# First block normalised by VectorE, first weight piece split in halves, two low parts moved to GpSimd

## The chip, the cores and the metric

One core of a Trainium2 chip runs the whole program in one launch. Its engines run side by side, each in the order of its own instruction list, and wait for each other by semaphores: TensorE (PE, with its weight loads as PEld), VectorE (DVE), ScalarE (ACT), GpSimd (POOL) and the queue of SyncE (SP), which issues most of the transfers. GpSimd issues transfers of its own. The metric is the device time in microseconds (us) of one execution, as the median of several runs.

## The reference

The program is one macaron layer on 4096 tokens (2 x 2048) of width 512: half a mixture-of-experts feed-forward, a state-space (Mamba-2) layer, and half a feed-forward again with the same weights.

```
x = x + 0.5 * ffn(layernorm(x))      # called "a" below
x = x + mamba(layernorm(x))          # "m"
x = x + 0.5 * ffn(layernorm(x))      # "b"

def ffn(x):                          # 64 experts of width 128, 4 per token, at most 64 tokens each
    scores = softmax(x @ router_w.T);  pick 4 per token;  gather, silu(gate) * up, down, scatter-add
    sg, su = x @ sh_gate_w, x @ sh_up_w               # shared part, width 2 x 512 = 1024
    return routed + (silu(sg) * su) @ sh_down_w
```

The change touches only the beginning of the first feed-forward.

## The kernel before, in words

Float32 products are made of three TensorE passes. Each operand is kept as a high part (a ScalarE copy into a reduced type) and a low part (the difference, one subtraction); `three` (L766 to L769) adds high times high, high times low and low times high.

**Stages of the first feed-forward.** Tokens of the shared part go in 16 blocks of 256 (`BS`), those of the router in 8 blocks of 512 (`BR`). The shared weights, 128 x 12288, arrive in six pieces of 128 x 2048, in the order 0, 1, 4, 2, 3, 5; a piece is known here by its place o in that order. Every piece lands in one of three staging buffers (`stage`, o = 0 to 5 use buffers 0, 1, 2, 0, 1, 2), ScalarE makes its high part (`split`, L610 to L616), VectorE its low part (`split`, L968 to L971), and only then may SyncE load the next piece into the same buffer (`load_piece`, L404 to L408).

**Start.** SyncE loads the first rows, piece 0, further rows, the router weights, pieces 1 and 2 and the block `xs` 0. VectorE takes mean and variance of the first 256 rows (`norm_first(0)`), GpSimd their inverse deviation (`inv_std`), and ScalarE normalises them in two passes per tile, one for the mean and one for the scale (`normed`, L618 to L635). TensorE turns them (`turn_s`), ScalarE and VectorE make the two parts of the turned rows (`turned_s`), and the first products of gate and up follow (`gate_or_up`). The engines' lists at the start read, in order:

```
SP    rows 0a, piece 0, rows 0b, router, pieces o = 1, 2, xs 0, pieces o = 3, 4, 5, xs 1, xr 1
ACT   split(0), normed(0), turned_s x2, split(1), split(2), split(3), r_both, silu(0), turned_r(0,0),
      split(4), split(5), product_hi(0), turned_r(0,1), silu(1), turned_r(0,2), ...
DVE   norm_first(0), split(0), turned_s x2, split(1), norm_first(1), norm_apply(0), split(2), split(3),
      r_both, product(0), turned_r(0,0), split(4), split(5), product_lo(0), turned_r(0,1), turned_r(0,2), ...
PE    turn_s x2, gate(0), up(0), turn_r(0,0), turn_r(0,1), logits(0,0), gate(1), turn_r(0,2), logits(0,1), up(1), ...
POOL  constants, zeros, inv_std(0) x2, the clearing of slot_rows (waits for all six low parts), inv_std(1), ...
```

**Router rows.** `norm_apply` makes the normalised rows `hr` of a router block. TensorE turns them in four groups into one PSUM tile `p_x0` (`turn_r`), so that group k + 1 waits until ScalarE and VectorE have read group k (`turned_r`, both engines; TensorE waits for `htr_ready`).

**The clearing.** GpSimd issues one transfer of 8336 KB of zeros into `slot_rows` (L543) once all low parts are made.

The second feed-forward runs the same code with `prior` set; its early part is interleaved with the end of the state-space layer. Semaphores of the first feed-forward are used again there.

## Time and profile before

| | |
|---|---|
| time, median of 3 runs | 2319.41 us (2318.42 to 2331.59) |
| span of the profiled execution, first to last instruction | 2318.1 us |
| TensorE busy | 2261.7 us (98%) |
| VectorE busy | 1364.6 us (59%) |
| ScalarE busy | 883.8 us (38%) |
| GpSimd busy | 692.8 us (30%) |
| mean granted TensorE clock | 0.992 |
| chain that ended last | TensorE 87%, DMA 7%, VectorE 3% |

The profiled execution is one of its own; its span is the time from its first to its last instruction, 1.3 us below the median of the runs. Busy time counts instructions that compute; a matmul's end is modelled, so successive matmuls overlap in the records and their pitch, the distance of their starts, tells more than their durations. In a timeline row stand the start, the time from that start to the end of the row's last instruction, the engine and line, what is written from what, how many instructions were merged, and in brackets the engine's idle time before it with what ended it.

### The profile page before, as it was taken

How to read it: one execution, taken by the hardware profiler on the slowest of the kernel's cores; microseconds unless marked ns; L12 is line 12 of the kernel's file. 1: busy time of each engine (PE TensorE's matmuls, PEld its weight loads, DVE VectorE, ACT ScalarE, POOL GpSimd, SP SyncE). 2: the span in 40 equal slices, each digit the busy share in tenths (PEclk: the TensorE clock that was granted, in tenths of full speed). 3: DMA queues.
4: the chain of work that ended last, by engine and by line, in shares of the span. 5: the costliest groups of instructions: out<-in, count | busy, mean ns of one | idle time of the engine just before them, and what ended most of it. 6: DMA issues, size and time to landing. Idle time of an engine off the chain costs nothing.

```text
span 2318.1 us, 41268 instructions
## 1 busy us (share of the span) xinstructions
PE 2261.7 (98%) x16412; PEld 1999.8 (86%) x16412; DVE 1364.6 (59%) x3200; ACT 883.8 (38%) x1562; POOL 692.8 (30%) x534
## 2 busy tenths in 40 slices
PE   6999999999999999999999999999999999999996
PEld 6999999777798899989889988998989999777785
DVE  6777762222327777777777777778776763223221
ACT  5232221233336455445455555555322221233230
POOL 1244443112221333333222232321144444112131
PEclk9999999999999999999999999999999999999998
DMA  8876424999854111111111111114385623889948
GB/s 268 267 256 217 154 93 156 304 277 284 245 112 134 39 28 28 29 28 28 29 28 28 28 29 34 32 41 154 134 294 186 224 75 106 310 275 286 280 81 175
DMA packets 129279, 334.73 MB, mean 144 GB/s; under 512 B 24450, under 2 KB 45186, under 8 KB 118400
## 3 DMA queue, kind: packets, MB, share of 16 engines
q1 hardware_dynamic: 80592, 236.63, 28.6%
q0 software_dynamic: 48496, 95.46, 18.2%
q8 instruction: 131, 2.15, 0.4%
q14 instruction: 60, 0.49, 0.1%
HBM read 218.25 MB, written 172.77 MB: 169 GB/s over the span
## 4 chain that ended last, share of the span: by engine, by line
PE 87%; DMA 7%; DVE 3%; issue 1%; ACT 1%; SPq 0%; POOLq 0%; DVEq 0%; POOL 0%; ACTq 0%
PE m_p_ab L1679 5%; PE m_p_ab L1680 4%; PE m_p_ab L1681 4%; DMA out<-b_y,b_row_no 4%; PE m_p_x L1679 3%; PE m_p_x L1681 3%; PE m_p_x L1680 3%; PE p_up_a L767 3%; PE p_x_a L871 3%; PE m_p_y L1799 2%; PE p_gate_a L767 2%; PE m_p_y L1800 2%; PE p_up_a L769 2%; PE p_up_a L768 2%; PE p_gate_a L768 2%; PE p_gate_a L769 2%
## 5 line engine op out<-in xcount | busy, mean ns | idle before, releaser
L1995 DVE SCALAR_TENSOR_TENSOR m_xt<-m_ssm,m_convw,m_xt 128x256 f32<-128x256 f32 x384 | 212.0, 565 | 57.7 <-ACT m_ssm L1546 48.5
L503 POOL DMA_INDIRECT slot_rows<-a_hr,a_slot_now x128 | 128.5, 1004 | 141.5 <-PE p_gate_a L769 91.5
L503 POOL DMA_INDIRECT slot_rows<-b_hr,b_slot_now x128 | 128.4, 1003 | 139.4 <-PE p_gate_b L769 90.5
L1679 PE MATMUL m_p_ab<-m_ht_hi,m_wi_b_hi 128*128 128x256 f32 x576 | 163.5, 284 | 1.8 <-ACT m_ssm L1546 1.8
L1680 PE MATMUL m_p_ab<-m_ht_lo,m_wi_b_hi 128*128 128x256 f32 x576 | 160.4, 279 | 0.0
L1681 PE MATMUL m_p_ab<-m_ht_hi,m_wi_b_lo 128*128 128x256 f32 x576 | 160.3, 278 | 0.0
L767 PE MATMUL p_gate_a<-a_hts_hi,a_w_hi 128*128 128x256 f32 x512 | 148.3, 290 | 1.8 <-DVE a_hts_lo L1066 1.8
L1452 POOL TENSOR_TENSOR m_state_dec<-m_state,m_etot 128x1024 f32<-128x1024 f32 x31 | 74.0, 2388 | 252.4 <-ACT m_etot L1562 252.4
L767 PE MATMUL p_gate_b<-b_hts_hi,b_w_hi 128*128 128x256 f32 x512 | 146.5, 286 | 0.4 <-DVE b_hts_lo L1066 0.4
L767 PE MATMUL p_up_a<-a_hts_hi,a_w_hi 128*128 128x256 f32 x512 | 145.6, 284 | 0.0
L767 PE MATMUL p_up_b<-b_hts_hi,b_w_hi 128*128 128x256 f32 x512 | 145.5, 284 | 0.0
L769 PE MATMUL p_gate_a<-a_hts_hi,a_w_lo 128*128 128x256 f32 x512 | 144.9, 283 | 0.0
L768 PE MATMUL p_gate_a<-a_hts_lo,a_w_hi 128*128 128x256 f32 x512 | 144.9, 283 | 0.0
L769 PE MATMUL p_gate_b<-b_hts_hi,b_w_lo 128*128 128x256 f32 x512 | 143.4, 280 | 0.0
L768 PE MATMUL p_gate_b<-b_hts_lo,b_w_hi 128*128 128x256 f32 x512 | 143.3, 280 | 0.0
L769 PE MATMUL p_up_a<-a_hts_hi,a_w_lo 128*128 128x256 f32 x512 | 143.1, 279 | 0.0
L769 PE MATMUL p_up_b<-b_hts_hi,b_w_lo 128*128 128x256 f32 x512 | 143.0, 279 | 0.0
L768 PE MATMUL p_up_a<-a_hts_lo,a_w_hi 128*128 128x256 f32 x512 | 143.0, 279 | 0.0
L768 PE MATMUL p_up_b<-b_hts_lo,b_w_hi 128*128 128x256 f32 x512 | 142.9, 279 | 0.0
L1072 DVE TENSOR_TENSOR b_prod<-b_silu,p_up_b 128x512 f32<-128x512 f32 x64 | 44.0, 688 | 155.5 <-PE p_up_b L769 154.4
L1072 DVE TENSOR_TENSOR a_prod<-a_silu,p_up_a 128x512 f32<-128x512 f32 x64 | 44.0, 688 | 139.4 <-PE p_up_a L769 138.1
L1544 ACT ACTIVATE m_xt<-m_p_ab,m_convb,m_convw 128x256 f32<-128x256 f32 x128 | 72.2, 564 | 129.2 <-PE m_p_ab L1681 129.2
(376 smaller groups left out, 7354.8 us busy)
## 6 DMA issues: line engine op xcount, KB each, us to landing
a_ew<-in_ew SPq DMA_DIRECT2D x32, 1536.0 KB, 7.7
b_ew<-in_ew SPq DMA_DIRECT2D x32, 1536.0 KB, 8.0
after_ffn<-a_zeros POOLq DMA_DIRECT2D x6, 2048.0 KB, 9.2
out<-b_zeros POOLq DMA_DIRECT2D x6, 2048.0 KB, 9.9
slot_rows<-a_zeros POOLq DMA_DIRECT2D x1, 8336.0 KB, 39.1
a_rows<-slot_rows SPq DMA_DIRECT2D x32, 260.5 KB, 8.4
b_rows<-slot_rows SPq DMA_DIRECT2D x32, 260.5 KB, 8.8
m_x<-after_ffn SPq DMA_DIRECT2D x16, 512.0 KB, 3.6
```

The costliest lines, as they stand in the source:

```text
L503: g_.indirect_dma_start(out=xg, out_offset=bass.IndirectOffsetOnAxis(ap=slot_now[r % HR][:, at:at + 1], axis=0), in_=hr[r % HR][:, j, :], ...
L767: t.matmul(out, l_hi, r_hi_, start=first, stop=False)
L768: t.matmul(out, l_hi, r_lo_, start=False, stop=False)
L769: return t.matmul(out, l_lo, r_hi_, start=False, stop=last)
L871: mm = t.matmul(p_x1[e * CAP:(e + 1) * CAP, 0:2 * F], xt[:, q % 2, k, e * CAP:(e + 1) * CAP], w[q % EU][:, e, k * 2 * F:(k + 1) * 2 * F], ...
L1072: v.tensor_tensor(prod[:, i % 2, :, :], silu[:, i % 2, :, :], p_up[:, :, :], ALU.mult).then_inc(prod_ready, 1)
L1452: g.tensor_tensor(state_dec[:], state[:], etot[:, j, :].unsqueeze(2).to_broadcast([P, NH, HP]), ALU.mult).then_inc(state_dec_ready, 1)
L1544: a.activation(xt[:, m, :], ab_of(J_SSM[m])[:, 0:BM], ACT.Identity, bias=convb[:, m:m + 1], scale=convw[:, m, HALO:CONV]).then_inc(tap_rea ...
L1679: t.matmul(out, l_hi, r_hi_, start=first, stop=False)
L1680: t.matmul(out, l_hi, r_lo_, start=False, stop=False)
L1681: return t.matmul(out, l_lo, r_hi_, start=False, stop=last)
L1995: ins_ = v.scalar_tensor_tensor(xt[:, m, :], ssm[:, m, i:i + BM], convw[:, m, i:i + 1], xt[:, m, :], ALU.mult, ALU.add)
```

## The change

ScalarE no longer normalises the first block: `normed(0)` leaves its list, and VectorE does it with one instruction per tile (`norm_shared`: subtract the mean, multiply by the inverse deviation), right after `norm_first(0)`. VectorE's subtraction for piece o = 0 is cut into two halves of 1024 columns, one before and one after its two `turned_s`; TensorE's first product waits for the first half only, its second for both. The low parts of o = 3 and o = 5 (`by_pool`) are made by GpSimd, right after the inverse deviations and ahead of the clearing; VectorE skips them. The waits on low parts count the two engines apart (`split_done`). SyncE's load of `xr` for block 1 waits for `hs_ready` in place of `hs_mid`, and the counts of `hs_mid` (`mids`) leave out the first block. For the second feed-forward `by_pool` is empty.

```
--- before.py
+++ after.py
@@ -277,6 +277,7 @@
 
         piece_loaded = [sem(f"piece_loaded{i}") for i in range(3)]
         small_loaded, w_hi_done, w_lo_done, r_split = sem("small_loaded"), sem("w_hi_done"), sem("w_lo_done"), sem("r_split")
+        w_lo_half, w_lo_pool = sem("w_lo_half"), sem("w_lo_pool")
         zeros_set, slots_cleared, acc_cleared = sem("zeros_set"), sem("slots_cleared"), sem("acc_cleared")
         xs_loaded, x_stored = [sem(f"xs_loaded{u}") for u in range(XB)], sem("x_stored")
         late_loaded = sem("late_loaded")
@@ -314,6 +315,15 @@
         norms = lambda at: at // TS + 1 if at < TR else at // TR + 2
         uses = lambda o: slot_of[:o + 1].count(slot_of[o])
 
+        by_pool = [] if prior else [3, 5]
+
+        def split_done(o):
+
+            on_pool = o in by_pool
+            return (w_lo_pool if on_pool else w_lo_done), len([e for e in range(o + 1) if (e in by_pool) == on_pool])
+
+        mids = lambda b: (own(b) - (0 if prior else 1)) * TS
+
 
         stored = lambda r: r - FROM_MEMORY[0] // 2 + 1 if 2 * r in FROM_MEMORY else 0
         own = lambda b: len([e for e in range(b + 1) if e not in FROM_MEMORY])
@@ -403,7 +413,7 @@
 
             def load_piece(o):
                 if uses(o) > 1:
-                    sp.wait_ge(w_lo_done, max(e for e in range(o) if slot_of[e] == slot_of[o]) + 1)
+                    sp.wait_ge(*split_done(max(e for e in range(o) if slot_of[e] == slot_of[o])))
                 i = order[o]
                 sp.dma_start(stage[slot_of[o]], shw[:, i * PIECE:(i + 1) * PIECE]).then_inc(piece_loaded[slot_of[o]], 16)
 
@@ -447,13 +457,14 @@
                         load_piece(o)
                         if o == 2:
                             load_xs(0)
-                    sp.wait_ge(w_lo_done, PIECES - 1)
+                    sp.wait_ge(*split_done(3))
+                    sp.wait_ge(*split_done(4))
                     load_xs(1)
                 for b in range(NS):
                     if b + 1 < NR:
                         sp.wait_ge(hr_ready, (b + 1) * TR)
                         if b == 0 and not prior:
-                            sp.wait_ge(hs_mid, TS)
+                            sp.wait_ge(hs_ready, TS)
                         sp.dma_start(xr[:], src_r[b + 1]).then_inc(xr_loaded, 16)
                     if b < NR:
                         store_turned(b, 0)
@@ -529,6 +540,11 @@
                 pool.dma_start(acc[first:first + rows, :], acc[HALF + first:HALF + first + rows, :], accum_op=ALU.add,
                                max_dma_last_dim=8192).then_inc(done, 16)
 
+            def split(o):
+                cols = slice(order[o] * PIECE, (order[o] + 1) * PIECE)
+                pool.wait_ge(w_hi_done, o + 1)
+                g_.tensor_tensor(w_lo[:, cols], stage[slot_of[o]], w_hi[:, cols].bitcast(F32), ALU.subtract).then_inc(w_lo_pool, 1)
+
             def early():
                 inv_std(0)
 
@@ -537,9 +553,12 @@
                 pool.wait_ge(zeros_set, 1)
                 if not prior:
                     inv_std(0)
+                for o in by_pool:
+                    split(o)
                 if clear_slots:
                     n = SLOTS // P
-                    pool.wait_ge(w_lo_done, PIECES)
+                    pool.wait_ge(w_lo_pool, len(by_pool))
+                    pool.wait_ge(w_lo_done, PIECES - len(by_pool))
                     pool.dma_start(xg.rearrange("(p a) d -> p (a d)", p=P).rearrange("p (n m) -> p n m", n=n),
                                    zeros[:, :].unsqueeze(1).to_broadcast([P, n, ROW])).then_inc(slots_cleared, 16)
                 inv_std(1)
@@ -581,7 +600,7 @@
                 if f.follow:
                     f.follow.pool.first()
                 add_block(NS - 3, ALL_ADDED)
-                pool.wait_ge(hs_mid, own(NS - 1) * TS)
+                pool.wait_ge(hs_mid, mids(NS - 1))
                 last = xs[:, (NS - 1) % XB, :, :]
                 pool.dma_start(last, acc_s[NS - 1], accum_op=ALU.add).then_inc(last_read, 16)
                 if merge_all:
@@ -617,10 +636,7 @@
 
             def normed(b):
                 rows_of = xs[:, b % XB, :, :]
-                if b == 0 and not prior:
-                    rows_of = xr
-                else:
-                    act.wait_ge(*loaded(b))
+                act.wait_ge(*loaded(b))
                 act.wait_ge(mean_ready, norms(b * TS))
                 act.wait_ge(rstd_ready, norms(b * TS))
                 wait(act, ts_full, 2 * own(b) - 2)
@@ -630,7 +646,7 @@
                                  bias=neg_mean[:, at:at + 1]).then_inc(hs_mid, 1)
                 for j in range(TS):
                     at = b * TS + j
-                    act.wait_ge(hs_mid, own(b) * TS - TS + j + 1)
+                    act.wait_ge(hs_mid, mids(b) - TS + j + 1)
                     a.activation(hs[:, j, :], hs[:, j, :], ACT.Identity,
                                  scale=rstd[:, at:at + 1]).then_inc(hs_ready, 1)
 
@@ -713,7 +729,6 @@
             def program():
                 if not prior:
                     split(0)
-                    normed(0)
                     turned_s(0, 0)
                     turned_s(0, 1)
                     act.wait_ge(c.built, c.BUILT)
@@ -787,10 +802,15 @@
                     else:
                         pe.wait_ge(hts_ready, 2 * own(b))
                 if g == 0 and b == 0:
-                    pe.wait_ge(w_lo_done, order.index(u) + 1)
+                    if i == 0 and not prior:
+                        pe.wait_ge(w_lo_half, 1)
+                    else:
+                        pe.wait_ge(*split_done(order.index(u)))
                 wait(pe, free, i)
                 for m in range(2):
                     n = 2 * u + m
+                    if i == 0 and g == 0 and m == 1 and not prior:
+                        pe.wait_ge(*split_done(0))
                     if g == 0 and m == 1 and turns_product(3 * i) is not None:
                         turn_prod(turns_product(3 * i))
                     for k in range(KD):
@@ -802,7 +822,7 @@
                 b, u = divmod(i, UN)
                 pe.wait_ge(act_ready, i + 1)
                 if b == 0 and u % 2 == 0:
-                    pe.wait_ge(w_lo_done, order.index(UN + u // 2) + 1)
+                    pe.wait_ge(*split_done(order.index(UN + u // 2)))
                 if u == 0:
                     wait(pe, acc_ready, b * TS)
                     if prior and b == 0:
@@ -966,9 +986,25 @@
                 dve.wait_ge(dve_step, steps[0])
 
             def split(o):
+                if o in by_pool:
+                    return
                 cols = slice(order[o] * PIECE, (order[o] + 1) * PIECE)
                 dve.wait_ge(w_hi_done, o + 1)
                 v.tensor_tensor(w_lo[:, cols], stage[slot_of[o]], w_hi[:, cols].bitcast(F32), ALU.subtract).then_inc(w_lo_done, 1)
+
+            def split_half(half):
+
+                cols = slice(half * PIECE // 2, (half + 1) * PIECE // 2)
+                dve.wait_ge(w_hi_done, 1)
+                v.tensor_tensor(w_lo[:, cols], stage[0][:, cols], w_hi[:, cols].bitcast(F32),
+                                ALU.subtract).then_inc(w_lo_done if half else w_lo_half, 1)
+
+            def norm_shared():
+
+                dve.wait_ge(rstd_ready, 1)
+                for j in range(TS):
+                    v.tensor_scalar(hs[:, j, :], xr[:, j, :], mv[:, j, 0:1], rstd[:, j:j + 1],
+                                    ALU.subtract, ALU.mult).then_inc(hs_ready, 1)
 
             def norm_stats(r):
                 if r == 0:
@@ -1138,9 +1174,11 @@
             def program():
                 if not prior:
                     norm_first(0)
-                    split(0)
+                    norm_shared()
+                    split_half(0)
                     turned_s(0, 0)
                     turned_s(0, 1)
+                    split_half(1)
                     split(1)
                     norm_first(1)
                     dve.wait_ge(c.built, c.BUILT)
```

## Rows read from the trace of the kernel before

**Rows 1.** The page: its head, then busy time, share and instructions of TensorE.
```profile
span 2318.1 us, 41268 instructions
PE 2261.7 (98%) x16412; PEld 1999.8 (86%) x16412; DVE 1364.6 (59%) x3200; ACT 883.8 (38%) x1562; POOL 692.8 (30%) x534
```

**Rows 2.** Waits of TensorE, whole span: waiter, releaser, us in total, times, longest.
```profile
PE p_ts_a L778 <- ACT a_hs L634: 11.5, 1, 11.5
PE p_x_a L823 <- DVE a_htr_lo L1008: 7.9, 4, 5.4
```

**Rows 3.** Timeline of TensorE, 14 to 36 us.
```profile
14.83 0.58 PE L767 MATMUL p_gate_a<-a_hts_hi,a_w_hi 128*128 128x256 f32 x1 [1.41 <-DVE a_hts_lo L1066]
...
28.82 1.09 PE L823 MATMUL p_x_a<-ident,a_hr 128*128 128x128 f32 x4 [5.44 <-DVE a_htr_lo L1008]
...
33.12 0.35 PE L767 MATMUL p_gate_a<-a_hts_hi,a_w_hi 128*128 128x256 f32 x1
...
34.45 0.28 PE L769 MATMUL p_gate_a<-a_hts_hi,a_w_lo 128*128 128x256 f32 x1
35.48 0.63 PE L823 MATMUL p_x_a<-ident,a_hr 128*128 128x128 f32 x4 [0.75 <-DVE a_htr_lo L1008]
```

**Rows 4.** Busy time by engine, 28 to 30 us; last three: clock, DMA share, GB/s.
```profile
28.00:30.00 2.00, 1.18 (x5) 1.21 (x6) 2.00 (x3) 0.10 (x1) 0.00 (x0) 0.50 0.55 229
```

**Rows 5.** Timeline of ScalarE, 13 to 32 us.
```profile
13.95 1.90 ACT L616 ACTIVATE a_w_hi<-a_xs 128x2048 fp32r<-128x2048 f32 x1
...
19.25 1.92 ACT L616 ACTIVATE a_w_hi<-a_hr 128x2048 fp32r<-128x2048 f32 x1 [1.60 <-DMA a_hr<-in_shw]
...
29.90 1.91 ACT L616 ACTIVATE a_w_hi<-a_hr 128x2048 fp32r<-128x2048 f32 x1 [4.08 <-DMA a_hr<-in_shw]
```

**Rows 6.** Timeline of VectorE, 15 to 35 us.
```profile
15.89 2.29 DVE L971 TENSOR_TENSOR a_w_lo<-a_xs,a_w_hi 128x2048 fp32r<-128x2048 f32 x1 [1.11 <-ACT a_w_hi L616]
...
20.75 1.92 DVE L1002 TENSOR_SCALAR a_hr<-a_xr,a_mv,a_rstd 128x512 f32<-128x512 f32 x4 [0.82 <-POOL a_rstd L495]
...
22.66 4.48 DVE L971 TENSOR_TENSOR a_w_lo<-a_hr,a_w_hi 128x2048 fp32r<-128x2048 f32 x2
...
28.00 0.68 DVE L1008 TENSOR_TENSOR a_htr_lo<-p_x_a,a_htr_hi 128x512 fp32r<-128x512 f32 x1
...
34.05 0.68 DVE L1077 TENSOR_TENSOR a_act_lo<-a_prod,a_act_hi 128x512 fp32r<-128x512 f32 x1
```

**Rows 7.** Timeline of SyncE's queue: issue of pieces o = 1 and o = 5.
```profile
3.33 0.45 SPq L408 DMA_DIRECT2D a_xs<-in_shw  x1
...
24.97 0.33 SPq L408 DMA_DIRECT2D a_hr<-in_shw  x1
```

**Rows 8.** Transfers issued from 3.2 to 3.6 us: KB each, us to landing.
```profile
a_xs<-in_shw SPq DMA_DIRECT2D x1, 1024.0 KB, 9.7
```

**Rows 9.** Timeline of GpSimd, 19 to 35 us.
```profile
19.94 0.70 POOL L495 TENSOR_TENSOR a_rstd<-a_var_eps,neg_half 128x2 f32<-128x2 f32 x1 [12.77 <-DVE a_var_eps L993]
34.46 1.87 POOL L543 DMA_DIRECT2D slot_rows<-a_zeros  x1 [13.82 <-DVE a_w_lo L971]
```

**Rows 10.** Timeline of GpSimd in the state-space layer, at 803 us.
```profile
803.43 2.64 POOL L1466 TENSOR_TENSOR m_cdec<-m_cdec,m_ct 128x1024 f32<-128x1024 f32 x1 [2.77 <-ACT m_cdec L1572]
```

**Rows 11.** Timeline of VectorE from 803.84 us.
```profile
803.86 3.01 DVE L1995 SCALAR_TENSOR_TENSOR m_xt<-m_ssm,m_convw,m_xt 128x256 f32<-128x256 f32 x2
```

**Rows 12.** Lines 1995 and 1452 alone: durations in ns, least/median/most.
```profile
L1995 DVE SCALAR_TENSOR_TENSOR m_xt<-m_ssm,m_convw,m_xt x384: 474/485/2506, 728.6 to 1571.7; 128x256 f32<-128x256 f32 x192
...
L1452 POOL TENSOR_TENSOR m_state_dec<-m_state,m_etot x31: 1899/2355/2882, 749.3 to 1551.4; 128x1024 f32<-128x1024 f32 x31
```

**Rows 13.** The page's transfers: KB each, us from issue to landing.
```profile
slot_rows<-a_zeros POOLq DMA_DIRECT2D x1, 8336.0 KB, 39.1
```

**Rows 14.** Queues from 31 to 38 us: packets, MB, share; q1 is SyncE's.
```profile
q1 hardware_dynamic: 989, 1.96, 85.9%
```

**Rows 15.** Timeline of ScalarE at 77 us.
```profile
76.98 0.60 ACT L661 ACTIVATE a_htr_hi<-p_x_a 128x512 fp32r<-128x512 f32 x1 [1.42 <-DMA turned_rows<-a_htr_lo]
```

More of the change, by code:

```diff
@@ L279, in ffn @@
         small_loaded, w_hi_done, w_lo_done, r_split = sem("small_loaded"), sem("w_hi_done"), sem("w_lo_done"), sem("r_split")
+        w_lo_half, w_lo_pool = sem("w_lo_half"), sem("w_lo_pool")
         zeros_set, slots_cleared, acc_cleared = sem("zeros_set"), sem("slots_cleared"), sem("acc_cleared")
@@ L315, in ffn, with split_done @@
         uses = lambda o: slot_of[:o + 1].count(slot_of[o])
+        by_pool = [] if prior else [3, 5]
+        def split_done(o):
+            on_pool = o in by_pool
+            return (w_lo_pool if on_pool else w_lo_done), len([e for e in range(o + 1) if (e in by_pool) == on_pool])
+        mids = lambda b: (own(b) - (0 if prior else 1)) * TS
         stored = lambda r: r - FROM_MEMORY[0] // 2 + 1 if 2 * r in FROM_MEMORY else 0
@@ L405, in load_piece @@
                 if uses(o) > 1:
-                    sp.wait_ge(w_lo_done, max(e for e in range(o) if slot_of[e] == slot_of[o]) + 1)
+                    sp.wait_ge(*split_done(max(e for e in range(o) if slot_of[e] == slot_of[o])))
                 i = order[o]
@@ L449, in program @@
                             load_xs(0)
-                    sp.wait_ge(w_lo_done, PIECES - 1)
+                    sp.wait_ge(*split_done(3))
+                    sp.wait_ge(*split_done(4))
                     load_xs(1)
@@ L455, in program @@
                         if b == 0 and not prior:
-                            sp.wait_ge(hs_mid, TS)
+                            sp.wait_ge(hs_ready, TS)
                         sp.dma_start(xr[:], src_r[b + 1]).then_inc(xr_loaded, 16)
@@ L530, in merge, with split @@
                                max_dma_last_dim=8192).then_inc(done, 16)
+            def split(o):
+                cols = slice(order[o] * PIECE, (order[o] + 1) * PIECE)
+                pool.wait_ge(w_hi_done, o + 1)
+                g_.tensor_tensor(w_lo[:, cols], stage[slot_of[o]], w_hi[:, cols].bitcast(F32), ALU.subtract).then_inc(w_lo_pool, 1)
             def early():
@@ L539, in program @@
                     inv_std(0)
+                for o in by_pool:
+                    split(o)
                 if clear_slots:
                     n = SLOTS // P
-                    pool.wait_ge(w_lo_done, PIECES)
+                    pool.wait_ge(w_lo_pool, len(by_pool))
+                    pool.wait_ge(w_lo_done, PIECES - len(by_pool))
                     pool.dma_start(xg.rearrange("(p a) d -> p (a d)", p=P).rearrange("p (n m) -> p n m", n=n),
@@ L583, in program @@
                 add_block(NS - 3, ALL_ADDED)
-                pool.wait_ge(hs_mid, own(NS - 1) * TS)
+                pool.wait_ge(hs_mid, mids(NS - 1))
                 last = xs[:, (NS - 1) % XB, :, :]
@@ L619, in normed @@
                 rows_of = xs[:, b % XB, :, :]
-                if b == 0 and not prior:
-                    rows_of = xr
-                else:
-                    act.wait_ge(*loaded(b))
+                act.wait_ge(*loaded(b))
                 act.wait_ge(mean_ready, norms(b * TS))
@@ L632, in normed @@
                     at = b * TS + j
-                    act.wait_ge(hs_mid, own(b) * TS - TS + j + 1)
+                    act.wait_ge(hs_mid, mids(b) - TS + j + 1)
                     a.activation(hs[:, j, :], hs[:, j, :], ACT.Identity,
@@ L789, in gate_or_up @@
                 if g == 0 and b == 0:
-                    pe.wait_ge(w_lo_done, order.index(u) + 1)
+                    if i == 0 and not prior:
+                        pe.wait_ge(w_lo_half, 1)
+                    else:
+                        pe.wait_ge(*split_done(order.index(u)))
                 wait(pe, free, i)
@@ L793, in gate_or_up @@
                     n = 2 * u + m
+                    if i == 0 and g == 0 and m == 1 and not prior:
+                        pe.wait_ge(*split_done(0))
                     if g == 0 and m == 1 and turns_product(3 * i) is not None:
@@ L804, in down @@
                 if b == 0 and u % 2 == 0:
-                    pe.wait_ge(w_lo_done, order.index(UN + u // 2) + 1)
+                    pe.wait_ge(*split_done(order.index(UN + u // 2)))
                 if u == 0:
@@ L968, in split @@
             def split(o):
+                if o in by_pool:
+                    return
                 cols = slice(order[o] * PIECE, (order[o] + 1) * PIECE)
@@ L971, in split, with split_half, norm_shared @@
                 v.tensor_tensor(w_lo[:, cols], stage[slot_of[o]], w_hi[:, cols].bitcast(F32), ALU.subtract).then_inc(w_lo_done, 1)
+            def split_half(half):
+                cols = slice(half * PIECE // 2, (half + 1) * PIECE // 2)
+                dve.wait_ge(w_hi_done, 1)
+                v.tensor_tensor(w_lo[:, cols], stage[0][:, cols], w_hi[:, cols].bitcast(F32),
+                                ALU.subtract).then_inc(w_lo_done if half else w_lo_half, 1)
+            def norm_shared():
+                dve.wait_ge(rstd_ready, 1)
+                for j in range(TS):
+                    v.tensor_scalar(hs[:, j, :], xr[:, j, :], mv[:, j, 0:1], rstd[:, j:j + 1],
+                                    ALU.subtract, ALU.mult).then_inc(hs_ready, 1)
             def norm_stats(r):
@@ L1140, in program @@
                     norm_first(0)
-                    split(0)
+                    norm_shared()
+                    split_half(0)
                     turned_s(0, 0)
                     turned_s(0, 1)
+                    split_half(1)
                     split(1)
```

1 line of the change is left out of this document (removed).

## Prediction

> **What bounds the kernel now.** I read the page first: TensorE is busy 2261.7 of 2318.1 us [rows 1], so a change elsewhere counts only where TensorE stands still or slows. The list of its waits shows where: 11.5 us before its first transposes, and 7.9 us in four waits for the low parts of turned router rows [rows 2]. The timeline of TensorE places them [rows 3]: products start at 14.83; then 5.44 us of idling end at 28.82 (`turn_r(0,1)`) and 0.75 us at 35.48 (`turn_r(0,2)`). From there to the end of the block no wait stands. So the change is worth what it does to the instant 35.48. TensorE also pays for idling: after those 5.44 us the granted clock was 0.50 [rows 4], the lower level of 1.2 GHz, until the row at 33.12, 4.3 us after the restart.
>
> The other timelines say what sets 35.48. VectorE's list runs almost without a gap from 15.89 [rows 6]: the low parts of o = 1, the statistics, four normalising steps from 20.75, two low parts from 22.66, then the turned rows at 28.00. The issue of o = 5 at 24.97 [rows 7] follows the first of those two low parts; ScalarE gets the piece at 29.90 [rows 5]; VectorE's `product_lo(0)` starts at 34.05 [rows 6], and the low part of the turned rows that releases TensorE stands behind it. From its start to TensorE's are 1.43 us.
>
> **Part 1: normalising on VectorE, and the halves.** Two VectorE steps cost about half of the 1.92 us of four [rows 6] and replace four ScalarE passes; half a low part stands ahead of TensorE's first product in place of a whole one. I estimate the first products some 3 us ahead of 14.83. But ScalarE's next copy (o = 1) began at 13.95 [rows 5] and can't begin before the piece lands, at 3.33 + 9.7 = 13.0 [rows 7, 8]. So 0.94 us is all that VectorE's list gains: `split(1)` 14.95, `norm_apply(0)` 19.81, `split(2)` 21.72. The issue of o = 3 waits for the second half, about 1.6 us later than for the whole low part; the transfers ahead of it cover that, and ScalarE gets it at 19.25 as before [rows 5]. If that cover were short, its lateness falls on GpSimd (rival 1). TensorE's first products then end earlier, only to wait for VectorE's rows. The new wait of SyncE on `hs_ready` is met long before its turn: nothing.
>
> **Part 2: two low parts on GpSimd.** No row has this subtraction there. The nearest is GpSimd's product of two 128x1024 arrays: 2.64 us at 803.43 [rows 10], of which 0.43 pass until VectorE's next instruction at 803.86 [rows 11]; so 2.2 alone, 4.4 for 2048 columns. I take 4.5, with 3.8 (twice the least, 1.899 [rows 12]) and 5.3 (twice 2.64) as ends. What it does to VectorE weighs more. Of VectorE's two instructions at 803.86, which take 3.01 us together, one has the usual 0.48 [rows 11, 12]; the other took 2.5, as long as GpSimd was at work, and it ended 0.28 us behind GpSimd. Both instructions read two arrays from SBUF, as a low part does. So I let such a VectorE instruction stand still while GpSimd subtracts, and let one that reads an array from PSUM run on.
>
> The page "SBUF — State Buffer" of the Trainium skill (section "Who interferes with whom") has the same as a rule, an exclusive lock for the whole instruction, and the rows agree (2.5 against 0.48 us). It adds that a tensor_scalar can enter a mode that takes the lock too; no row here shows that. By it GpSimd's first subtraction would wait for VectorE's fourth normalising step, 0.4 us, and the sum below would be 7.5 in place of 7.1.
>
> **The sum, along the new path.** ScalarE's copy of o = 3 ends at 19.25 + 1.92 = 21.17 [rows 5]; GpSimd starts at 21.25, being free since its second inverse deviation (0.70 us from 19.94, now 19.0 [rows 9]). VectorE comes to `split(2)` at 21.72, 0.47 us too late, and stands still until GpSimd ends:
> - GpSimd 21.25 + 4.5 = 25.75; VectorE's blocked `split(2)` ends 0.2 earlier plus 2.29 [rows 6], 27.85, where it was 24.95.
> - The staging buffer is free only then: o = 5 is issued at 27.87 (was 24.97), reaches ScalarE 4.93 later [rows 5, 7] at 32.8, and is copied by 34.7.
> - GpSimd takes its low part, 34.8 to 39.3. ScalarE's `product_hi(0)` ends 0.6 after that copy, so `product_lo(0)`, two SBUF arrays again, is held from 35.3 to 39.15.
> - 1.43 later TensorE gets `turn_r(0,2)`: 40.6 against 35.48, **5.1 us late**. Each 0.1 us of GpSimd's subtraction counts twice here.
> - In between, `turned_r(0,0)` comes at 28.7 in place of 28.00, TensorE's gate(1), which ended 5.6 us after the restart at 28.82 (34.45 [rows 3]), ends at 35.2, and TensorE idles 5.4 us, as long as the idling after which the clock was 0.50 [rows 4]. Restarted at the lower level for 4.3 us, it does 2.15 us of work there: about **2.0 us** more, since a little of it is not matmul time.
>
> Sum 7.1 us. VectorE's `split(4)` lies in the time it would else wait in. `load_xs(1)` and the rows behind it on SyncE's queue are issued at about 31.6, 0.7 later than now, and wanted after 42. On GpSimd the clearing stands behind both subtractions: issued at 39.4, not 34.46 [rows 9], with the 39.1 us of [rows 13] it lands at 78.5. What waited for it, the stores of turned rows ahead of ScalarE's wait at 76.98 [rows 15], is itself 7 us later, so nothing is added. `inv_std(1)` behind it is needed after 50. The second feed-forward is unchanged; two more semaphores to clear cost nothing that I can name. TensorE has no slack after 40 us to win it back: 2318.1 + 7.1 = 2325.2 for this execution, and the median stands 1.3 above the span: **2326.5 us**. With 3.8 and 5.3 for the subtraction the 7.1 become 5.7 and 8.7; if the clock stays up, 5.1, at the least 3.7. So this case spans 2323 to 2328.
>
> **Rival 1: VectorE is first.** If o = 3 comes 0.5 us later (its later issue) or VectorE's list is 0.5 ahead, `split(2)` holds GpSimd off. Then o = 5 is issued at 24.0, GpSimd runs 24.0 to 28.5 beside the held `r_both`, and its second subtraction waits for `split(4)` until 32.0 and ends at 36.5; `product_lo(0)` at 36.35, TensorE at 37.8: 2.3 us late, idle 2 us, clock untouched. 2321.7. The margin of 0.47 is small, but both its ends are measured.
>
> **Rival 2: faster, since the engines don't hold each other up.** It decides at 21.7 us: if `split(2)` takes 2.29 us beside GpSimd, VectorE has shed 2.2 us and `turned_r(0,0)` comes 3.2 earlier, TensorE's `turn_r(0,2)` 2.8 earlier. That is not kept. The stores that ScalarE waits for at 76.98 [rows 15] lie behind the clearing; SyncE's 1.96 MB filled the engines alone until 38 [rows 14], now they would be gone by 36, and the clearing, issued at 35.5 behind GpSimd's second subtraction, would start about 37.2, not 38.3. Gain 1.1: 2318.3. For it speaks that no row has this very pair of instructions side by side; against it, 2.5 us against 0.48.
>
> **Rival 3: GpSimd is much slower**, since no row shows it write the reduced type. At 7 us each, the sum grows by twice 2.5: 2331.5.
>
> **How the numbers follow.** Forecast 0.66, rival 1 0.14, rival 2 0.12, rival 3 0.08. The forecast's 2323 to 2328 and rival 1 hold 0.80; with a microsecond for the scatter of runs (two of the three lie 1 us apart) the range is 2320.5 to 2329. A change of 1% (23 us), about what a measurement of this kernel can tell from none, is beyond every case: within it 0.98, faster and slower 0.01 each.
>
> **What would show it.** In the changed profile: TensorE's first products near 12; ScalarE's o = 1 copy at 13.0; GpSimd's subtractions of about 4.5 us at 21.3 and 34.8; VectorE's low part of o = 2 recorded with 6 us, not 2.29, and `product_lo(0)` with some 4 us; `turn_r(0,2)` at 40 to 41, and clock 0.50 behind it. Wrong would be: low parts of 2.29 us beside GpSimd (rival 2), or o = 2 ahead of GpSimd (rival 1).

## The result, and the profile after

The changed kernel takes 2329.82 us, the median of 22 runs; the kernel before, run beside it, 2321.78. The ratio is 1.0028 with a 95% interval of 1.0016 to 1.0040, so some 6.5 us more (3.7 to 9.3; the two medians lie 8.0 apart). One of the 22 runs of the kernel before took 10326.67 us and is left out of the ratio. The forecast, 2326.5 against the 2319.4 known then, was a ratio of 1.0031. By the measured ratio 2319.41 becomes 2325.9, inside the stated 2320.5 to 2329; the median of 2329.82 itself lies above that range, as the kernel before, too, measured 2.4 us more than was known then. The profiled execution of the changed kernel took 2327.96 us, its span is 2326.3, which is 8.2 above the span of before.

The head of the page after, and TensorE's share (before: [rows 1]):

```profile
span 2326.3 us, 41270 instructions
...
PE 2265.0 (97%) x16412; PEld 2002.7 (86%) x16412; DVE 1368.8 (59%) x3201; ACT 882.2 (38%) x1558; POOL 704.0 (30%) x536
```

TensorE has the same instructions and 3.3 us more of busy time; the other 4.9 us are waits. The three costliest of them, from the list of TensorE's waits after (before: [rows 2]):

```profile
PE p_x_a L843 <- DVE a_htr_lo L1044: 9.8, 4, 5.2
PE p_ts_a L793 <- DVE a_hs L1006: 8.4, 1, 8.4
PE p_x_a L843 <- DVE a_hr L1038: 6.2, 1, 6.2
```

The start of the block is 3.1 us earlier than before (8.4 for 11.5). In its place stands a wait that the kernel before did not have, 6.2 us for the normalised router rows `hr`, and the waits for the low parts of turned rows grew from 7.9 to 9.8. TensorE's timeline after places them (before: [rows 3]):

```profile
11.74 0.58 PE L782 MATMUL p_gate_a<-a_hts_hi,a_w_hi 128*128 128x256 f32 x1 [1.41 <-DVE a_hts_lo L1102]
...
26.20 1.12 PE L843 MATMUL p_x_a<-ident,a_hr 128*128 128x128 f32 x4 [6.24 <-DVE a_hr L1038]
...
30.09 1.09 PE L843 MATMUL p_x_a<-ident,a_hr 128*128 128x128 f32 x4 [2.78 <-DVE a_htr_lo L1044]
...
41.00 1.09 PE L843 MATMUL p_x_a<-ident,a_hr 128*128 128x128 f32 x4 [5.22 <-DVE a_htr_lo L1044]
...
46.16 0.60 PE L843 MATMUL p_x_a<-ident,a_hr 128*128 128x128 f32 x4
```

Two rows of before, `turn_r(0,0)` and `turn_r(0,3)`:

```profile
22.73 0.66 PE L823 MATMUL p_x_a<-ident,a_hr 128*128 128x128 f32 x4
...
39.16 0.60 PE L823 MATMUL p_x_a<-ident,a_hr 128*128 128x128 f32 x4
```

The products begin at 11.74 in place of 14.83, and that is all gone again at the second row: `turn_r(0,0)` comes at 26.20, where it was 22.73 before. `turn_r(0,1)` is 1.3 us late, `turn_r(0,2)` 5.5 (41.00 for 35.48), and `turn_r(0,3)` 7.0 (46.16 for 39.16). VectorE's timeline after says why (before: [rows 6]):

```profile
15.13 2.29 DVE L993 TENSOR_TENSOR a_w_lo<-a_xs,a_w_hi 128x2048 fp32r<-128x2048 f32 x1 [2.31 <-ACT a_w_hi L635]
...
20.00 6.15 DVE L1038 TENSOR_SCALAR a_hr<-a_xr,a_mv,a_rstd 128x512 f32<-128x512 f32 x4 [0.83 <-POOL a_rstd L506]
...
26.14 2.28 DVE L993 TENSOR_TENSOR a_w_lo<-a_hr,a_w_hi 128x2048 fp32r<-128x2048 f32 x1
...
35.74 4.51 DVE L1113 TENSOR_TENSOR a_act_lo<-a_prod,a_act_hi 128x512 fp32r<-128x512 f32 x1 [3.59 <-ACT a_act_hi L667]
40.18 0.68 DVE L1044 TENSOR_TENSOR a_htr_lo<-p_x_a,a_htr_hi 128x512 fp32r<-128x512 f32 x1
```

The four normalising steps, 1.92 us before, take 6.15; `product_lo(0)`, 0.68 us before, takes 4.51. `split(2)` at 26.14 takes its usual 2.28. The same timeline of VectorE, asked from 21.5 us, shows the fourth normalising step by itself:

```profile
21.37 4.77 DVE L1038 TENSOR_SCALAR a_hr<-a_xr,a_mv,a_rstd 128x512 f32<-128x512 f32 x1
```

GpSimd's timeline after (before: [rows 9]):

```profile
21.36 4.50 POOL L546 TENSOR_TENSOR a_w_lo<-a_hr,a_w_hi 128x2048 fp32r<-128x2048 f32 x1 [1.48 <-ACT a_w_hi L635]
35.20 4.51 POOL L546 TENSOR_TENSOR a_w_lo<-a_hr,a_w_hi 128x2048 fp32r<-128x2048 f32 x1 [9.33 <-ACT a_w_hi L635]
40.03 1.88 POOL L562 DMA_DIRECT2D slot_rows<-a_zeros  x1 [0.32 <-POOL a_w_lo L546]
```

Put the two side by side. GpSimd starts at 21.36 and ends at 25.86; VectorE's step starts 0.01 us behind it, at 21.37, and ends at 26.14. GpSimd starts again at 35.20 and ends at 39.71; `product_lo(0)` starts at 35.74 and ends at 40.25. Each time VectorE's short instruction ends 0.3 to 0.5 us behind GpSimd's long one.

What is late because of the first hold-up is the issue of o = 5, which waits for `split(2)`. SyncE's queue after (before: 24.97 [rows 7]):

```profile
28.44 0.33 SPq L418 DMA_DIRECT2D a_hr<-in_shw  x1
```

ScalarE's timeline after, the copies of o = 1, 3 and 5 (before: [rows 5]):

```profile
13.19 1.91 ACT L635 ACTIVATE a_w_hi<-a_xs 128x2048 fp32r<-128x2048 f32 x1 [2.22 <-DMA a_xs<-in_shw]
...
19.38 1.91 ACT L635 ACTIVATE a_w_hi<-a_hr 128x2048 fp32r<-128x2048 f32 x1 [1.88 <-DMA a_hr<-in_shw]
...
33.20 1.91 ACT L635 ACTIVATE a_w_hi<-a_hr 128x2048 fp32r<-128x2048 f32 x1 [3.46 <-DMA a_hr<-in_shw]
```

And the clock behind the 5.22 us wait, from busy time by engine in stretches after (the last three columns are granted clock, DMA share, GB/s; before: [rows 4] for its one slow restart):

```profile
41.00:42.00 1.00, 1.00 (x5) 1.00 (x6) 0.00 (x0) 0.00 (x0) 0.91 (x1) 0.50 0.06 16
42.00:44.00 2.00, 2.00 (x9) 1.81 (x9) 0.69 (x1) 0.60 (x1) 0.00 (x0) 0.50 0.73 254
...
44.40:45.00 0.60, 0.60 (x7) 0.60 (x7) 0.00 (x0) 0.00 (x0) 0.00 (x0) 1.00 1.01 236
```

From the restart at 41.00 until about 44.3 the granted clock is 0.50 (1.2 GHz). Before, the stretch from `turn_r(0,2)` to `turn_r(0,3)` took 3.68 us; now it takes 5.16, so the clock costs 1.5 us. (The slow stretch behind `turn_r(0,1)` [rows 4] is there in both kernels.)

From there the shift stays. `turn_r(1,3)` starts at 85.19 (78.52 before, 6.7 late), and an early ScalarE row of the state-space layer, a table load, at 731.67 (724.75, 6.9 late). At that layer's end, 1580.33 against 1572.15, the two profiled executions are 8.2 apart, and so are the spans. The last 1.3 us arise in code that the change does not touch; the profiled executions below gain or lose up to 2.6 us between `turn_r(1,3)` and their ends, so nothing shows these 1.3 us to be an effect of the change.

### The profile page after: what moved, and what is told of

Same layout as the page of the kernel before. It is cut to its first block, busy times and chain, and to the rows that moved or that the text cites. A ratio compares the mean times of both kernels' runs of the same rounds, so it can differ in the third digit from the quotient of the medians.

```text
span 2326.3 us, 41270 instructions
## 1 busy us (share of the span) xinstructions
PE 2265.0 (97%) x16412; PEld 2002.7 (86%) x16412; DVE 1368.8 (59%) x3201; ACT 882.2 (38%) x1558; POOL 704.0 (30%) x536
## 4 chain that ended last, share of the span: by engine, by line
PE 93%; DVE 3%; DMA 2%; ACT 1%; issue 1%; SPq 0%; DVEq 0%; POOL 0%; ACTq 0%; POOLq 0%
PE m_p_ab L1717 5%; PE m_p_ab L1718 4%; PE m_p_ab L1719 4%; PE m_p_x L1717 3%; PE m_p_x L1719 3%; PE m_p_x L1718 3%; PE p_up_b L782 3%; PE p_up_a L782 3%; PE p_gate_b L782 3%; PE p_x_b L891 3%; PE p_x_a L891 3%; PE p_gate_b L783 3%; PE p_gate_b L784 3%; PE p_up_b L784 3%; PE p_up_b L783 3%; PE m_p_y L1837 2%
## 6 DMA issues: line engine op xcount, KB each, us to landing
slot_rows<-a_zeros POOLq DMA_DIRECT2D x1, 8336.0 KB, 34.6
```

## The experiments

The theory: GpSimd's subtraction, which reads two SBUF arrays, holds up VectorE instructions that run beside it, once at 21.4 us and once at 35 us, both on the way to `turn_r(0,2)`; the wait so made is long enough for the clock to fall. Rivals: part 1 of the change does the harm (SyncE's order, the late issue of o = 3); GpSimd merely makes the low parts later than VectorE did, with no hold-up; any work of GpSimd holds VectorE up, whatever it reads. Eight kernels were run. In the table the instants are the starts of TensorE's transposes in the profiled execution, in us.

| kernel | median us | ratio to before (95%) | span | `turn_r(0,1)` | `turn_r(0,2)` | `turn_r(1,3)` |
|---|---|---|---|---|---|---|
| before | 2321.78 | 1 | 2318.1 | 28.82 | 35.48 | 78.52 |
| after | 2329.82 | 1.0028 (1.0016 to 1.0040) | 2326.3 | 30.09 | 41.00 | 85.19 |
| part 1 alone | 2321.02 | 0.9992 (0.9975 to 1.0009) | 2319.4 | 27.82 | 34.35 | 77.26 |
| GpSimd part alone | 2330.27 | 1.0043 (1.0028 to 1.0058) | 2326.3 | 30.81 | 41.85 | 87.29 |
| only o = 3 on GpSimd | 2324.45 | 1.0011 (0.9997 to 1.0025) | 2322.4 | 30.02 | 38.78 | 83.29 |
| only o = 5 on GpSimd | 2324.09 | 1.0009 (0.9994 to 1.0024) | 2320.5 | 27.93 | 36.78 | 79.69 |
| GpSimd only writes | 2323.48 | 1.0016 (0.9995 to 1.0037) | 2317.3 | 29.56 | 36.23 | 79.10 |
| o = 3 subtracted twice | 2325.78 | 1.0005 (0.9980 to 1.0031) | 2320.3 | 32.11 | 38.70 | 81.67 |
| new order, o = 5 late on GpSimd | 2319.54 | 0.9989 (0.9972 to 1.0007) | 2313.6 | 25.65 | 30.75 | 74.52 |
| new order, all on VectorE | 2318.83 | 0.9986 (0.9965 to 1.0007) | 2314.4 | 25.95 | 31.91 | 75.37 |

Each ratio is to runs of the kernel before made beside that kernel (their medians: 2321.78 for after, 2323.02 for the next four rows, 2322.93 for the last four), so it is not the quotient of two medians in the table. The intervals reach 2.8 to 5.9 us to either side; what is smaller is read from the instants, which are those of one execution each.

**Part 1 alone.** Both subtractions go back to VectorE, the rest of the change stays.

```
-        by_pool = [] if prior else [3, 5]
+        by_pool = [] if prior else []
...
-                    pool.wait_ge(w_lo_pool, len(by_pool))
+                    wait(pool, w_lo_pool, len(by_pool))
```

> Only the first part of the change: VectorE normalises the first block and makes the first low part in halves; all six low parts stay with VectorE. Theory (GpSimd's subtractions hold VectorE up): without them the loss is gone and VectorE's list is 0.7 to 0.9 us ahead of before; turn_r(0,2) starts on TensorE at 34.7 (35.5 before, 41.0 after the change), time 0 to 1 us below before. Rival (the first part does harm: o = 3 is issued 1.6 us later, its landing slips): ScalarE's copy of o = 3 later than 19.4, turn_r(0,2) well behind 35.5.

VectorE's and then TensorE's timeline of this kernel:

```profile
19.75 1.92 DVE L1038 TENSOR_SCALAR a_hr<-a_xr,a_mv,a_rstd 128x512 f32<-128x512 f32 x4 [0.82 <-POOL a_rstd L506]
...
32.92 0.68 DVE L1113 TENSOR_TENSOR a_act_lo<-a_prod,a_act_hi 128x512 fp32r<-128x512 f32 x1
```

```profile
34.35 0.63 PE L843 MATMUL p_x_a<-ident,a_hr 128*128 128x128 f32 x4 [1.33 <-DVE a_htr_lo L1044]
```

Without GpSimd's subtraction the four steps take 1.92 us and `product_lo(0)` 0.68. TensorE is at `turn_r(0,2)` 1.13 us earlier than before; the products that began 3 us early bought no more than that. ScalarE's copy of o = 3 starts at 19.14, not later than before (19.25). So part 1 does no harm, and the first rival falls. In the whole time 1.1 us can't be told from nothing (0.9975 to 1.0009).

**The GpSimd part alone.** ScalarE normalises the first block as before, and o = 0 is subtracted whole; o = 3 and o = 5 stay on GpSimd.

```
-        mids = lambda b: (own(b) - (0 if prior else 1)) * TS
+        mids = lambda b: own(b) * TS
...
+                    normed(0)
...
-                    norm_shared()
-                    split_half(0)
+                    split(0)
...
-                    split_half(1)
```

> Only the second part: GpSimd makes the low parts of o = 3 and 5, all else as before. Theory: GpSimd starts at 21.3, when VectorE has done one or two of its four normalising steps (from 20.75), and holds the rest up for 4.5 us; o = 5 is issued near 29, product_lo(0) is held again, turn_r(0,2) at 41.5 to 42, time 8 us above before, 1 above the change. Rival (the first part does the harm): as before, 35.5 and no difference.

VectorE's timeline of this kernel:

```profile
20.73 6.13 DVE L1042 TENSOR_SCALAR a_hr<-a_xr,a_mv,a_rstd 128x512 f32<-128x512 f32 x4 [0.82 <-POOL a_rstd L506]
...
36.59 4.50 DVE L1117 TENSOR_TENSOR a_act_lo<-a_prod,a_act_hi 128x512 fp32r<-128x512 f32 x1 [3.74 <-ACT a_act_hi L670]
```

Its third normalising step by itself, and GpSimd's timeline:

```profile
21.65 4.75 DVE L1042 TENSOR_SCALAR a_hr<-a_xr,a_mv,a_rstd 128x512 f32<-128x512 f32 x1
```

```profile
21.41 4.71 POOL L546 TENSOR_TENSOR a_w_lo<-a_hr,a_w_hi 128x2048 fp32r<-128x2048 f32 x1 [0.79 <-ACT a_w_hi L635]
```

The two hold-ups are there in full, and the loss with them: 6.4 us at `turn_r(0,2)`, and 1.0043 in time. Here GpSimd began at 21.41, beside the second of the four steps, took 0.21 us longer than after (4.71 for 4.50), and it was the third step that stood still. The loss belongs to the GpSimd part, and it doesn't hang on the fourth step being the one that is met.

**Only o = 3, and only o = 5, on GpSimd.** One line each.

```
-        by_pool = [] if prior else [3, 5]
+        by_pool = [] if prior else [3]
```

> The change, but GpSimd makes only the low part of o = 3; VectorE that of o = 5. Theory: one hold-up, of the fourth normalising step; o = 5 is issued at 28.4, VectorE makes its low part at 35.1 to 37.4, turn_r(0,2) at 38.9 (3.4 us behind before); TensorE idles 3 us ahead of it, so its clock may stay up: time 3.5 us above before, 5.5 if the clock falls. Rival (a hold-up costs nothing that VectorE would not have waited for anyway): 35 to 36.

```
-        by_pool = [] if prior else [3, 5]
+        by_pool = [] if prior else [5]
```

> The change, but GpSimd makes only the low part of o = 5; VectorE that of o = 3. Theory: up to o = 5 VectorE is 0.8 us ahead of before; GpSimd subtracts from 31.2 to 35.7, product_lo(0) is held until then, turn_r(0,2) at 36.9, 1.4 us behind before, no clock loss: time 1.5 us above before. Rival (all the harm is done by the second subtraction): 41.

With o = 3 alone, VectorE's timeline, and TensorE's:

```profile
19.93 6.14 DVE L1038 TENSOR_SCALAR a_hr<-a_xr,a_mv,a_rstd 128x512 f32<-128x512 f32 x4 [0.82 <-POOL a_rstd L506]
...
37.35 0.69 DVE L1113 TENSOR_TENSOR a_act_lo<-a_prod,a_act_hi 128x512 fp32r<-128x512 f32 x1
```

```profile
38.78 0.63 PE L843 MATMUL p_x_a<-ident,a_hr 128*128 128x128 f32 x4 [3.45 <-DVE a_htr_lo L1044]
```

With o = 5 alone, VectorE's timeline, and TensorE's:

```profile
31.48 4.55 DVE L1113 TENSOR_TENSOR a_act_lo<-a_prod,a_act_hi 128x512 fp32r<-128x512 f32 x1 [1.50 <-ACT a_act_hi L667]
```

```profile
36.78 0.63 PE L843 MATMUL p_x_a<-ident,a_hr 128*128 128x128 f32 x4 [3.30 <-DVE a_htr_lo L1044]
```

Each subtraction makes its own hold-up and no other: with o = 3 there the four steps take 6.14 us and `product_lo(0)` 0.69, with o = 5 there `product_lo(0)` takes 4.55 and the steps 1.92. Counted from part 1 alone, `turn_r(0,2)` is 4.43 us late with the first and 2.43 with the second; the sum, 6.86, is what both together cost, 6.65. In the ratios it is the same (0.0019 and 0.0017 above part 1 alone, 0.0036 for both), though their intervals are too wide to show it by themselves.

The clock parts the two. With o = 5 alone it stayed at 1.00 through a wait of 3.30 us. With o = 3 alone, after a wait of 3.45 us, it was at 1.00 at the restart and fell behind it; stretches of this kernel (granted clock is third from the end):

```profile
38.00:40.00 2.00, 1.22 (x9) 1.16 (x10) 0.64 (x2) 0.55 (x1) 1.88 (x1) 1.00 0.80 301
40.00:42.00 2.00, 2.00 (x11) 2.00 (x11) 0.69 (x1) 0.04 (x1) 0.00 (x0) 0.50 0.70 246
```

So o = 3 alone is 6.03 us late at `turn_r(1,3)`, 1.6 more than at `turn_r(0,2)`, and o = 5 alone is 2.43 late at both. Why two waits of nearly one length end so differently is left open; in the first kernel TensorE had also stood still for 6.67 us until 26.13.

**GpSimd works without reading.** VectorE makes all low parts. In place of its first subtraction GpSimd sets 128x2048 elements of `w_lo` twice, in columns that VectorE fills later.

```
-                g_.tensor_tensor(w_lo[:, cols], stage[slot_of[o]], w_hi[:, cols].bitcast(F32), ALU.subtract).then_inc(w_lo_pool, 1)
+                for n in range(2):
+                    g_.memset(w_lo[:, 5 * PIECE:6 * PIECE].bitcast(F32), float(n)).then_inc(w_lo_pool, 1)
+                    pool.wait_ge(w_lo_pool, n + 1)
```

> VectorE makes all low parts; GpSimd, in the place of its first subtraction, only writes constants, twice 128x2048, into columns of w_lo that are made later (about 4 us from 21.3). Theory (an instruction of VectorE with two arrays from SBUF is held up by GpSimd's reading): the low parts of o = 2 and 3 keep 2.3 us each; whether a normalising step is held by writing is open (2 us at most); turn_r(0,2) at 34.4 to 36.4. Rival (any work of GpSimd holds VectorE up): VectorE held for 4 us, o = 5 issued at 28, turn_r(0,2) at 38.5.

GpSimd's timeline of this kernel, and VectorE's:

```profile
21.28 3.88 POOL L547 MEMSET a_w_lo<- 128x2048 f32 x2 [1.47 <-ACT a_w_hi L637]
```

```profile
19.93 3.48 DVE L1040 TENSOR_SCALAR a_hr<-a_xr,a_mv,a_rstd 128x512 f32<-128x512 f32 x4 [0.83 <-POOL a_rstd L506]
23.33 1.85 DVE L1042 TENSOR_SCALAR a_hr<-token_no 128x4 f32<-128x4 f32 x1
23.40 4.48 DVE L995 TENSOR_TENSOR a_w_lo<-a_hr,a_w_hi 128x2048 fp32r<-128x2048 f32 x2
```

The two fills last from 21.28 to 25.16. `split(2)` starts at 23.40, 1.76 us ahead of their end, and the pair of subtractions takes 4.48 us as in [rows 6]: a GpSimd that only writes does not hold up an instruction with two SBUF arrays. It does hold up the normalising step, which has one SBUF array and writes SBUF: 3.48 us for 1.92 up to the end of the first fill, and the small step of 128x4 elements is recorded with 1.85 us in place of 0.16 up to the end of the second. So "any GpSimd work holds everything" falls, and so does a theory of two-array instructions alone. `turn_r(0,1)` is 1.74 us behind part 1 alone; 1.56 of that is the held step, and 0.18 lay ahead of it (19.93 for 19.75). The whole time settles nothing here (0.9995 to 1.0037). A GpSimd that only reads was not run.

**The subtraction done twice.** VectorE makes all low parts, and GpSimd subtracts o = 3 besides, into columns that VectorE fills later. GpSimd takes no work away here; only its presence is added.

```
-                g_.tensor_tensor(w_lo[:, cols], stage[slot_of[o]], w_hi[:, cols].bitcast(F32), ALU.subtract).then_inc(w_lo_pool, 1)
+                g_.tensor_tensor(w_lo[:, 5 * PIECE:6 * PIECE], stage[slot_of[o]], w_hi[:, cols].bitcast(F32), ALU.subtract).then_inc(w_lo_pool, 1)
```

> VectorE makes all low parts, and GpSimd subtracts o = 3 once more, into columns of w_lo that are made later: the hold-up without its relief. Theory: VectorE's fourth normalising step or its low part of o = 2 is held until 25.8, o = 5 is issued at 28.4, turn_r(0,1) at 32.3 (27.8 with the first part alone), turn_r(0,2) at 38.8; time 3 to 5.5 us above before. Rival (the harm is that GpSimd takes longer for a low part that is waited for, not that VectorE is held up): as with the first part alone, 27.8 and 34.4.

VectorE's timeline of this kernel, and TensorE's:

```profile
19.80 6.15 DVE L1038 TENSOR_SCALAR a_hr<-a_xr,a_mv,a_rstd 128x512 f32<-128x512 f32 x4 [0.83 <-POOL a_rstd L506]
...
25.95 4.48 DVE L993 TENSOR_TENSOR a_w_lo<-a_hr,a_w_hi 128x2048 fp32r<-128x2048 f32 x2
```

```profile
38.70 0.63 PE L843 MATMUL p_x_a<-ident,a_hr 128*128 128x128 f32 x4 [0.51 <-DVE a_htr_lo L1044]
```

The hold-up alone, 4.23 us on the steps, makes `turn_r(0,2)` 4.35 late: the rival of a merely later low part falls. This also shows what moving o = 3 was worth at `turn_r(0,2)`: VectorE does it again here, and that row comes at 38.70, against 38.78 where GpSimd does it. Nothing, since the buffer for o = 5 comes free with `split(2)`, which stands ahead of o = 3 on VectorE's list in either case. (`turn_r(0,1)` does come 2.1 us earlier where GpSimd does it, and TensorE waits that time away ahead of `turn_r(0,2)`: 3.45 us against 0.51.) In the whole time 3 to 5.5 us were expected above before; the estimate is 1.2, and its interval (0.9980 to 1.0031) settles nothing.

**A new order on VectorE.** What then would help at `turn_r(0,2)`? In part 1 alone `product_lo(0)` stands behind `split(4)` and `split(5)`, and by that behind the transfer of o = 5. Two kernels put it ahead: VectorE does `split(2)`, `r_both`, `product(0)`, the first turned rows, `split(4)`, `product_lo(0)`, the second turned rows, and only then o = 3 and o = 5; ScalarE's copy of o = 5 moves behind its `turned_r(0,1)`. The clearing waits for five low parts and goes ahead of any subtraction on GpSimd. In the first, o = 5 is GpSimd's, behind the issue of the clearing; in the second all is VectorE's.

```
+                made = [e for e in (0, 1, 2, 4, 3, 5) if (e in by_pool) == on_pool]
+                return (w_lo_pool if on_pool else w_lo_done), made.index(o) + 1
...
+                if clear_slots:
+                    n = SLOTS // P
+                    pool.wait_ge(w_lo_done, 5)
...
                 for o in by_pool:
                     split(o)
-                if clear_slots:
...
-                    split(3)
...
-                            for o in late.get(u, []):
+                            for o in late.get(u, []) if prior else [4] if u == 0 else []:
...
+                        if b == 0 and u == 0 and not prior:
+                            split(3)
+                            split(5)
```

> First part, and another order: VectorE makes the low part of o = 4 ahead of o = 3, both behind turned_r(0,0), and turned_r(0,1) comes before o = 3; ScalarE copies o = 5 behind turned_r(0,1); the clearing is issued once o = 0 to 4 are done; GpSimd makes only the low part of o = 5, behind the issue of the clearing, when VectorE's next instructions read PSUM. Theory: GpSimd's 4.5 us (32.0 to 36.5) hold nothing up; turn_r(0,1) at 25.6, turn_r(0,2) at 31 to 32, no wait of TensorE there; the clearing starts 2 us earlier than before and bounds the gain: time 1.5 to 2.5 us below before. Rival (GpSimd's subtraction costs wherever it stands): 3 us more than the same order with VectorE alone.

> The order of the run before this one, with all low parts on VectorE (o = 3 and o = 5 behind turned_r(0,1)). Theory: turn_r(0,1) at 25.6, turn_r(0,2) at 31 to 32; time 1.5 to 2.5 us below before, the gain bounded by the clearing, whose transfer starts 2 us earlier. Rival (the gain at the start is lost again behind the clearing): ScalarE's wait for the stores of turned rows near 77 us as before, gain under 0.5 us.

With o = 5 late on GpSimd: GpSimd's timeline, then VectorE's beside it, then TensorE's, and the ScalarE row that waits for the stores of turned rows:

```profile
31.63 1.87 POOL L561 DMA_DIRECT2D slot_rows<-a_zeros  x1 [11.97 <-DVE a_w_lo L996]
33.45 4.72 POOL L548 TENSOR_TENSOR a_w_lo<-a_hr,a_w_hi 128x2048 fp32r<-128x2048 f32 x1
```

```profile
34.65 0.69 DVE L1111 TENSOR_TENSOR a_prod<-a_silu,p_up_a 128x512 f32<-128x512 f32 x1 [1.89 <-PE p_up_a L787]
36.52 0.69 DVE L1047 TENSOR_TENSOR a_htr_lo<-p_x_a,a_htr_hi 128x512 fp32r<-128x512 f32 x1 [1.18 <-ACT a_htr_hi L678]
37.13 1.59 DVE L1116 TENSOR_TENSOR a_act_lo<-a_prod,a_act_hi 128x512 fp32r<-128x512 f32 x1
```

```profile
30.75 0.60 PE L846 MATMUL p_x_a<-ident,a_hr 128*128 128x128 f32 x4
```

```profile
72.98 0.60 ACT L678 ACTIVATE a_htr_hi<-p_x_a 128x512 fp32r<-128x512 f32 x1 [2.22 <-DMA turned_rows<-a_htr_lo]
```

With all on VectorE, the timelines of GpSimd, TensorE and ScalarE:

```profile
31.92 1.87 POOL L561 DMA_DIRECT2D slot_rows<-a_zeros  x1 [11.95 <-DVE a_w_lo L996]
```

```profile
31.91 0.60 PE L846 MATMUL p_x_a<-ident,a_hr 128*128 128x128 f32 x4
```

```profile
73.84 0.60 ACT L678 ACTIVATE a_htr_hi<-p_x_a 128x512 fp32r<-128x512 f32 x1 [1.89 <-DMA turned_rows<-a_htr_lo]
```

TensorE has no wait at all at `turn_r(0,2)`, which comes 4.7 and 3.6 us ahead of before (3.6 and 2.4 ahead of part 1 alone). So the rival that GpSimd's subtraction costs 3 us wherever it stands falls. Beside GpSimd's subtraction (33.45 to 38.17) the two VectorE instructions with one array from PSUM take their usual 0.69 us, and `product_lo(1)`, with two from SBUF, is held until it ends at 38.72; nothing on TensorE waits for it. At `turn_r(1,3)` 4.0 and 3.2 us are kept, and the traces point to the clearing as the bound. ScalarE's wait for the stores of turned rows, 1.42 us before [rows 15], is 2.22 and 1.89 here. The clearing lands (issue plus its 39.1, 38.4 and 38.8 us) at 73.6 before and at 70.0 and 70.7 here, and in all three kernels the ScalarE row behind that wait starts 3.0 to 3.4 us later. Both kernels are faster than after (their intervals, up to 1.0007, lie below that of after, from 1.0016). Against before, the best estimate is 2.6 and 3.3 us gained, where 1.5 to 2.5 was expected, and neither interval leaves out zero.

## Why the prediction was right

**Part 1.** As worked out: the products start at 11.74 (near 12), the copy of o = 1 at 13.19 (13.0, when the piece lands), `split(1)` at 15.13 (14.95), o = 3 reaches ScalarE at 19.38 (19.25). The shift of VectorE's list, put at 0.94, is 0.76 in the profile of after and 1.01 in that of part 1 alone.

**GpSimd's two subtractions.** 4.50 and 4.51 us, where 4.5 was taken between 3.8 and 5.3. Rival 3, with 7 us, is out. The rows that the 4.5 came from wrote f32 [rows 10 to 12]; writing the reduced type costs nothing that shows beside them.

**Which instruction is held.** Here a step failed, though its price hardly did. The prediction let VectorE come to `split(2)` 0.47 us too late and stand still there, and let the normalising steps run beside GpSimd. It was the fourth normalising step that stood still, from 21.37 to 26.14, and `split(2)` ran unhindered. VectorE's list is held until the same GpSimd end either way, so o = 5 was issued at 28.44, only 0.57 later than the 27.87 of the sum: 0.11 is GpSimd's later start (21.36 for 21.25), the rest the held step, which has now to end before `split(2)` can begin. The prediction had not weighed this case, so that its price came out nearly the same is luck. But the normalised rows themselves came late with the held step, and TensorE's transposes `turn_r(0,0)` waited for them for 6.24 us. The prediction had TensorE wait there for VectorE's rows too, but put them at 21.7, and the kernel with part 1 alone shows a wait of 1.80 us. It cost nothing more at `turn_r(0,2)`, which hangs on o = 5, and it made the wait at `turn_r(0,1)` shorter (2.78).

The rule of the Trainium skill that the prediction quoted and kept out of its sum (the page "SBUF — State Buffer", section "Who interferes with whom": a tensor_scalar can enter a mode that takes the shared lock) agrees with this trace as far as the time goes, 4.77 us for 0.54; that a mode of VectorE is the cause, no run here shows. What the prediction made of it was the other half, that GpSimd would wait for VectorE; by the records GpSimd was first by 0.01 us. The same section of the Trainium skill also states that an instruction with two SBUF inputs is at odds with a GpSimd instruction that reads SBUF and not with one that only writes it; this agrees with the fills (4.48 us for two subtractions, as without them).

**Rivals 1 and 2.** Rival 1 had VectorE first, with `split(2)` holding GpSimd off; GpSimd was first after all, but by the records only by 0.01 us and not by the 0.47 counted, since the instruction at the edge was the normalising step and not `split(2)`. The chance of 0.14 came from the wrong pair. Rival 2 let the engines run side by side; 4.51 us for 0.68 at `product_lo(0)` says no. Its price, 1.1 us because the clearing would give the rest back, was not put to the test: where `turn_r(0,2)` did come early, the clearing was issued at 31.63 and 31.92 and not at 35.5. What those two kernels show speaks for its reasoning, for the clearing landed 3.5 and 2.8 us earlier than before, and 4.0 and 3.2 us were left at `turn_r(1,3)`.

**The second hold-up.** ScalarE got o = 5 at 33.20 (32.8), GpSimd began at 35.20 (34.8), `product_lo(0)` ended at 40.25, and TensorE had `turn_r(0,2)` at 41.00 (40.6). The 0.4 is there from ScalarE's copy on: it is the 0.57 of the first hold-up, less 0.17, since the piece reached ScalarE 4.76 us after its issue and not 4.93. That each hold-up counts by itself is what the two kernels with one subtraction show (4.43 and 2.43).

**The clock.** The wait ahead of 41.00 was 5.22 us (5.4), the restart was at 0.50 as forecast, and it came back after 3.3 us rather than 4.3. So this term is 1.5 us, not 2.0.

**The sum.** 5.5 and 1.5 are 7.0 us at `turn_r(0,3)`, against 5.1 and 2.0, together 7.1. That the total fits to 0.1 is luck, since 0.4 too little and 0.5 too much cancel. Downstream nothing was won back but 0.3 us: the clearing was issued at 40.03 (39.4) and took 34.6 us, not 39.1, and ScalarE no longer waits for the stores behind it. The 8.2 of the profiled spans holds 1.3 us from the untouched state-space layer; the ratio, 6.5 us, is nearer to the sum.

## What to carry to other kernels

Before moving work from VectorE to an idle GpSimd, list what VectorE will run in those microseconds: here each GpSimd subtraction of two SBUF arrays stopped a VectorE instruction of 0.5 to 0.7 us for some 4 us, and the second engine's time was paid for twice on one path. If the work is to go there all the same, put it where VectorE waits, reads PSUM, or does what nobody waits for, as in the new order with o = 5 late. And ask first whether the moved work is on the path at all: moving o = 3 was worth nothing at `turn_r(0,2)`, while the order with `product_lo(0)` ahead of a late transfer brought 2.4 us there over part 1 alone, with all low parts on VectorE.
